# Score runs of two heads issued together in the first attention of a fused transformer layer

## The reference

```python
q = (x @ Wq).reshape(B, N, h, dh).transpose(0, 2, 1, 3) * scale
k, v = (kv[..., :dh], kv[..., dh:])
sim = jnp.einsum('bhid,bjd->bhij', q, k)
sim = sim + bias.transpose(2, 0, 1)[None] * bias_scale
sim = jnp.where(causal[None, None], -jnp.finfo(sim.dtype).max, sim)
attn = jax.nn.softmax(sim, axis=-1)
out = jnp.einsum('bhij,bjd->bhid', attn, v)
```

## Time and profile before

| | before |
|---|---|
| median of three runs | 1132.87 us (1132.27 to 1138.27) |
| profiled execution, span in it | 1134.53 us, 1132.8 us |
| mean granted TensorE clock | 0.918 |
| TensorE (PE) busy, matmuls | 976.8 us, 6218 |
| VectorE busy | 766.6 us |
| ScalarE busy | 595.5 us |
| GpSimd busy | 331.5 us |
| first attention, from its first scores (23 us) to about | 540 us |

### The profile page before, as it was taken

How to read it: one execution, slowest core, us unless ns; L and a number is a source line. 1 busy time by engine, 2 the same in 40 slices (tenths; PEclk the granted TensorE clock), 3 DMA queues, 4 the chain that set the end, 5 groups by cost and what they waited for, 6 DMA issues and landing times. The chain is left out here.

```text
span 1132.8 us, 18698 instructions
## 1 busy us (share of the span) xinstructions
PE 976.8 (86%) x6218; PEld 628.0 (55%) x6218; DVE 766.6 (68%) x2268; ACT 595.5 (53%) x1176; POOL 331.5 (29%) x420
## 2 busy tenths in 40 slices
PE   6999999999999999999638567889999999997382
PEld 4766677676767666666437424344444444434372
DVE  6776757775777757675612699787988888854422
ACT  4766667675766657664212363415555555564120
POOL 3522122112222112210235006543454434311522
PEclk9999999999999999999659589868999999998586
DMA  6630000000000000000621100000000000001523
GB/s 209 133 86 2 1 2 1 1 1 1 2 1 1 1 1 2 1 1 1 180 64 38 38 0 1 1 1 1 1 2 1 1 2 1 1 1 43 164 58 94
DMA packets 49356, 32.25 MB, mean 28 GB/s; under 512 B 9147, under 2 KB 45932, under 8 KB 49260
## 3 DMA queue, kind: packets, MB, share of 16 engines
q1 hardware_dynamic: 47212, 26.78, 8.4%
q0 software_dynamic: 2048, 4.26, 1.1%
HBM read 21.44 MB, written 11.69 MB: 29 GB/s over the span
## 5 line engine op out<-in xcount | busy, mean ns | idle before, releaser
L618 ACT ACTIVATE attn_a_prob<-attn_a_score,attn_a_m_all 128x128 f32<-128x128 f32 (+7 forms) x256 | 188.8, 740 | 52.5 <-DVE attn_a_m_all L541 48.9
L968 ACT ACTIVATE attn_b_probT<-attn_b_st 128x1024 f32<-128x1024 f32 (+1 forms) x192 | 145.1, 808 | 131.7 <-PE attn_b_st L834 130.4
L537 DVE TENSOR_REDUCE attn_a_m_far<-attn_a_score 128x1 f32<-128x512 f32 (+3 forms) x192 | 105.7, 550 | 65.0 <-PE attn_a_score L449 62.8
L461 PE MATMUL attn_a_slot<-tab,attn_a_prob 128*128 128x128 f32 x1152 | 149.6, 274 | 0.0
L473 PE MATMUL attn_a_o<-attn_a_ptsb,Vd 128*64 128x512 f32 x288 | 140.6, 606 | 0.0
L473 PE MATMUL attn_a_o<-attn_a_ptsa,Vd 128*64 128x512 f32 x288 | 140.5, 606 | 0.0
L461 PEld LDWEIGHTS attn_a_slot<-tab,attn_a_prob 128*128 128x128 f32 x1152 | 132.0, 141 | 10.6 <-issue 3.2
L897 DVE CUSTOM_DVE_ANT_0 attn_b_slot<-attn_b_slot,later 128x128 f32<-128x128 f32 (+3 forms) x256 | 118.6, 522 | 18.7 <-PE attn_b_slot L809 18.5
L809 PE MATMUL attn_b_slot<-KS,attn_b_alone 128*128 128x512 f32 (+2 forms) x384 | 124.8, 421 | 3.6 <-POOL attn_b_alone L990 2.4
L627 ACT ACTIVATE attn_a_ptsa<-attn_a_slot 128x512 f32<-128x512 f32 x144 | 85.7, 595 | 65.2 <-PE attn_a_slot L461 64.8
L541 DVE CUSTOM_DVE_ANT_0 attn_a_score<-attn_a_score,bias_near,attn_a_m_far 128x256 f32<-128x256 f32 (+2 forms) x192 | 107.4, 559 | 7.0 <-DVE attn_a_m_far L537 0.2
(11 more groups left out here) (233 smaller groups left out, 1851.3 us busy)
## 6 DMA issues: line engine op xcount, KB each, us to landing
moe_weights_w<-in_L_ffn_w_dram SPq DMA_DIRECT2D x32, 256.0 KB, 4.2
to_experts<-xn SPq DMA_DIRECT2D x2, 1056.0 KB, 11.7
moe_experts_xe<-to_experts SPq DMA_DIRECT2D x16, 132.0 KB, 2.4
bias_by_query_and_key<-bias_by_distance SPq DMA_DIRECT2D x2, 1024.0 KB
bias_near<-bias_by_query_and_key SPq DMA_DIRECT2D x2, 1024.0 KB, 6.1
from_experts<-xn SPq DMA_DIRECT2D x2, 1024.0 KB, 11.6
moe_experts_back<-from_experts SPq DMA_DIRECT2D x8, 256.0 KB, 3.8
X<-in_L_attn_a_x_dram SPq DMA_DIRECT2D x2, 512.0 KB, 4.6
```

The lines of the kernel that those rows point to most:

```text
L461: ins = nc.tensor.transpose(dst[:, jj * P:(jj + 1) * P], probs(g)[:, 2 * jj + half, i * P:(i + 1) * P], ident[:, :])
L537: nc.vector.tensor_reduce(least, score[t % 2][:, at:at + nk - win], AX.X, ALU.min).then_inc(far_done, 1)
L618: nc.scalar.activation(probs(g)[:, j, 0:nk], score[t % 2][:, at:at + nk], ACT.Exp, bias=m_all[:, j:j + 1], scale=-1.0, accum_out=rowsum[g ...
L968: nc.scalar.activation(probT[n % 2][:, two, lo:], st[:, two, lo:], ACT.Exp, scale=-1.0).then_inc(exp_done, 1)
```

## The change

For the long groups TensorE issues the scores of two heads, j and j+1, in the even tick, and none in the odd tick. What follows scores in a tick keeps its place in the loop, so that the values tail of tick 0 and the turned blocks, values, queries, projection and R of both ticks come behind both score runs. Short groups and the lists of the other engines stay as they are. The number of instructions and the semaphore counts that they wait for are the same.

```diff
@@ -496,7 +496,11 @@
             for g, j in TICKS:
-                if g < GROUPS:
+                if g < GROUPS and is_long(g * HS):
+                    if j % 2 == 0:
+                        scores(g, j)
+                        scores(g, j + 1)
+                elif g < GROUPS:
                     scores(g, j)
                 if j == 0 and g >= 2:
                     for i in range((steps(g - 2) - 1) // 2 * 2, steps(g - 2)):
```

## The result

The changed kernel takes 1203.76 us in the median of four runs (1200.03 to 1205.47) against 1135.03 us of the kernel before (1132.27 to 1138.27): ratio 1.0605, 95% interval 1.0573 to 1.0637. Its profiled execution took 1205.47 us with a span of 1203.8, 71.0 more than the span of before.

What follows compares the result with a forecast made beforehand. The prediction took TensorE to bound the kernel. Stalls of 14.6 us per set over four sets gave 58 us, and 1132.87 + 58 = 1191 us, own range 1175 to 1205, 8-in-10 range 1168 to 1210.

Steps and rivals of the forecast that it cites:

- What bounds: Whole kernel: TensorE sets the pace, busy 86% of the span; VectorE and ScalarE are far from full.
- Idle time ahead of scores in a set: Sign in the four long tiles: TensorE's idle time waiting for exp rises from 3.0 to some 15 us per set.
- TensorE's busy time: Sign in the profile after: about the same as before, since no instruction is added or removed.
- Stall 1: S3 in long groups: exp(1) waits behind OT, release at +5.35 from S1's start, TensorE 1.6 us early.
- Stall 2: S7 in long groups: R's transposes to S7's release take 2.33 us, filled only by R and S6; 1.0 us stall.
- Stall 3: Seam to the next group: exp(6) behind a turned block's copy, release +3.26 from S7, 1.5 us wait against 0.6 before.
- the walk: Step-by-step tally of delays through four long groups of one set, each continuing from the one before, with own exp lengths.
- The sum without the clock: Long tiles 4 to 7: +4.1, +3.6, +3.3 and +3.6 us, 14.6 us per set, 58 us over four sets.
- adjacent runs: Paired score runs: a gain of 0.1 us taken where no stall stands between, 0 to 6 us over 64 pairs.
- The clock: Seams of long groups: stalls drop the clock, 1 to 1.7 us per fall, sixteen falls, 1205 to 1218 us; chance 0.08.
- the clock leaves 1.00: Sign of being wrong in the profile after: granted clock expected to stay at 1.00.
- Mild and faster case: Rivals: only S7 stalls remain, 1148 us, chance 0.10; cover suffices and only adjacency counts, 1127 us, chance 0.04.

Runs made afterwards that it cites:

- e5: The whole change, with VectorE's OT of the group two back behind the maximum of head 1 in long groups: 1177.0 us.
- e12: The whole change, with ScalarE copying R behind exp(5) instead of ahead of it in long groups: 1178.1 us.
- e4: Against the kernel before, only S6 and S7 issued together in long groups: 1148.7 us against 1130.3 of before.
- e7: The whole change, plus eight idle identity transposes ahead of S0 and eight ahead of S1 in tiles 5 and 7: 1189.6 us.
- e2: Against the kernel before, only S2 and S3 issued together in long groups: 1147.3 us against 1130.3 of before.
- e3: Against the kernel before, only S4 and S5 issued together in long groups: 1133.9 us against 1130.3 of before.
- e6: The whole change, with the values tail of the group two back ahead of S0 and S1 in long groups: 1167.5 us.
- e8: The whole change, with VectorE's and ScalarE's lists put in TensorE's order in long groups: 1155.6 us, 1.0228 of before.
- e11: The whole change with both e8's reordered lists and e6's values tail ahead of S0 and S1: 1165.5 us, 1.0251 of before.
- e1: Against the kernel before, only S0 and S1 issued together in long groups, values tail behind both: 1149.1 us against 1130.3 of before.

## Why the prediction came right, and where its sizes were off

**What bounds.** Right: TensorE sets the pace, so each wait of it counts in full. 1203.8 minus 1132.8 us of span is 71.0; the four sets, taken tile by tile like the second, give about 69 of it. Idle time ahead of scores in a set went from 3.0 to 15.0 us, as predicted. TensorE's busy time, which the prediction held to be about the same, went up by 20.9 us: about half is the slower matmuls at 1.2 GHz, and in e5, whose second set has no fall, a set still has 2.5 us more of it (80.6 against 78.1) than before, with no matmul added. So the waits cost more than the idle time in the rows says.

**Stall 1, S3 behind OT.** Right to the hundredth in tile 6 (OT at +2.15, release +5.34 against +5.35 predicted), and e5 shows the cause. (The rows named for the far maximum, 0.82 us behind its scores, are 0.85 apart; this chain doesn't use that distance, since the maximum comes behind OT.)

**Stall 2, S7 behind R.** Right: 0.85 us idle and the matmul's tail, against 1.0; e12 shows the cause.

**Stall 3, the seam.** 3.20 us from S7 to S0 against 3.26. Its cause, the copy ahead of exp(6), is argued and not shown, as it was not tested alone; e4, which has only this pair, shows the waits where the walk puts them.

**The sum without the clock.** 14.6 us a set predicted, 14.56 in e7; 3.93, 3.55, 3.36, 3.71 against 4.1, 3.6, 3.3, 3.6. The terms hold one by one too: idle ahead of S3 is 1.03, 1.27, 1.41 and 1.52 us against 1.3, 1.6, 1.6 and 1.8 in the walk, and a wait costs about 0.25 us more than its idle time (in e2 0.64 us idle ahead of S3 in tile 5 cost 0.89). The small errors cancelled in the sum: the walk gave adjacent runs 0.1 us where e3 shows nothing.

**The clock, the term that was mis-sized.** The forecast of 1191 us had it at zero and gave the case a chance of 0.08; "the clock leaves 1.00" was one of its own signs of being wrong. It came: seven stretches at 1.2 GHz instead of one in the first attention, at 1.6 to 1.7 us each some 10 us more, and 1191 + 10, with 2 us because the median of before is 1135.03 with its fourth run, not 1132.87, is near the 1204 measured. The price in the prediction (1 to 1.7 us per fall) was right; the number was not, seven and not sixteen. The time stayed inside 1168 to 1210 with some luck, since the width of that range was meant for errors of the stalls, which were small, and took in only the lower end of the clock case (from 1205 us). The rows had a hint: after a stretch with TensorE busy 2.66 of 4.00 us the clock fell, and my walk put stalls of 1.3, 0.9 and 1.6 us close together at the seam of tile 5. But no row could give the number of falls: with the same pauses ahead of S0 and S1 the change has seven at eight such seams (tiles 5 and 7 of four sets), e5 one and e12 one. The case deserved more than 0.08; seven was not to be read there.

**Mild and faster case.** Neither came. Stalls do not fall off, since each chain restarts from the last stalled score run, and e3 shows that pairing has no gain of its own.

## What to carry to other kernels

Grouping work of one kind on the engine that sets the pace changes what covers each of its waits: for every wait, list the blocks between the release that it needs and the place where it waits, before and after. Where other engines work through lists in a fixed order, an edit of one list makes the others deliver in the wrong order; follow each chain through them by hand, from rows. And where the sum brings stalls close together, add a term for the clock, as a range: here it was worth 10 us in one kernel and under 2 in others with the same pauses ahead of S0 and S1.

## What the runs showed of the hardware

A pause of 1 us ahead of S0 and another of 0.8 us ahead of S1 were followed at once, in seven of eight cases in the changed kernel, by a stretch at 1.2 GHz, in tiles where TensorE was busy for 21.1 of 24.2 and 26.4 of 29.6 us. Sets two to four repeat each other to 0.05 us, tile by tile, so the seven are fewer separate cases than they seem. It does not come each time: in the first set tile 5 of the changed kernel kept 2.4 GHz and cost 3.55 us instead of 5.20. And in e5 and e12, where a wait that lies behind these two is about 1 us shorter (S3 in e5, S7 in e12) and the two pauses are the same to 0.01 us, it came once in eight cases each: tile 5 of the first set in e5, tile 7 of the first set in e12. In the kernels where S0 and S1 wait less (e6, e7, e8, e11), and in e1 and e4, where only one of the two pauses is long, no long group has a fall. So the size of the pauses right ahead does not decide it alone; what does, these runs don't settle. Eight useless transposes in each of two waits of these groups went with a gain of about 1% of the time.

The Trainium skill, page "TensorE: Matmul & The Clock Gate", section "A second HAM failure mode: psum-queue depth-cycling", has frequent short idling between groups of matmuls as a cause of such swings. Here the trace agrees in part: granted clock 0.93 and 0.94 in tiles 5 and 7 of the change and 1.00 with the pauses filled, but also 1.00 in tile 5 of the second set of e5, with the pauses as they were.
